# Three accumulation tables in place of four in a graph-layer kernel on one Trainium2 core

## The chip, the core and the metric

The kernel runs on one core of a Trainium2 chip. The core has five engines with instruction streams of their own: TensorE (PE, with its weight loads shown as PEld), VectorE (DVE), ScalarE (ACT), GpSimd (POOL) and SyncE (SP), and 16 DMA engines that they share. Semaphores order the streams. The metric is the device time of one execution in microseconds (us), lower is better. Times of several executions are given as a median; the profile is of one execution.

## What is computed

A layer over 6250 nodes of 256 features and 100000 edges, in float32. Three branches are added: a message-passing branch, a linear attention branch and, last, a slice-attention branch. The change touches the first one. Cut to what matters:

```python
xn = layernorm(x)
filt = silu(edge_attr @ Wf1 + bf1) @ Wf2 + bf2          # 100000 x 256
msg = xn[dst] * filt
agg = segment_sum(msg, src, num_segments=6250)          # scatter-add by src
h = silu(agg @ Wu1 + bu1) @ Wu2 + bu2
bn = gamma * (h - mean(h)) * rsqrt(var(h) + eps) + beta  # over the nodes
x = x + (xn + bn) + attention(xn)                        # then the slice branch
```

Edges come sorted by dst, so a row of `agg` (by src) is hit by edges from all over the list.

## The kernel before

Six stages run one after the other, each a block that ends with a barrier over the engines: `opening`, `messages_and_attention`, `update_nodes`, `slice_tokens`, `slice_attention`, `slice_output`.

**opening** normalises the rows of x, writes them split in two float32r halves to DRAM, and prepares the attention. Between those seven stores SP issues the clearing of the tables (L254 to L262): each table of 6400 rows of 256 floats in DRAM is cleared by 8 DMAs of 800 KB, 32 in all with four tables, four or five behind each store.

**messages_and_attention** (L716) goes over NCH = 98 chunks of 1024 edges, 8 tiles of 128 edges each, so 784 tiles; work is in pairs of tiles, 4 to a chunk. PE makes filter and gathered rows, DVE multiplies them to messages, PE sums messages of equal src within a tile, ACT copies the sums of a pair to `summed` (`copy_sums`, L1050, instruction on L1056), DVE makes the row indices `out_idx` (L1166), and POOL adds each tile's 128 rows of 1 KB to a table in DRAM with one indirect accumulating DMA (`scatter`, L893, instruction on L903). An accumulating DMA reads, adds and writes; two of them in flight on one table could lose a sum, as both may hit the same row. So tile t goes to table `t % 4`, and before its issue POOL waits (L902) on the semaphore `added[k]` until the scatter four tiles earlier, on the same table, has landed. `out_ready` and `sum_ready` (L894, L895) are waited for once a pair, before its first (even) tile.

`summed` has two buffers of 8 tiles. ACT may copy a pair only when the scatters of the same tiles two chunks earlier have landed (L1052 to L1055), so the sums can run at most 16 tiles ahead of the scatters. PE's next `merge` (L961) waits for that copy (`sum_ready`), and the rest of PE, ACT and DVE stands in order behind it.

The stage ends when all scatters have landed (L923). The attention's output is computed alongside, in the places of `output`.

**update_nodes** (L1268) takes 49 tiles of nodes in 13 units of four (the last has one). SP loads a unit's rows of all tables to `part` (L1352: 52 loads, 48 of 512 KB and 4 of 128 KB), two units deep. POOL adds part 2 and part 3 (`late_sums`, L1510 to L1513); DVE adds part 1 to part 0 (L1536), waits for POOL (L1538) and adds part 2 (L1539). PE turns the sum (L1375), multiplies by Wu1 (L1387) and, a unit behind, by Wu2 (L1401); POOL's other work is `low_hidden` (L1518), and ACT and DVE (L1550, statistics of h) finish the unit. The order on DVE is: sums of unit u+1, their low halves, statistics of unit u-1.

Of the kernel before, what the change touches and what calls it, by code (L numbers as in the profile page):

```python
# [24 lines left out]
NODES, C = 6250, 256  # L25
# [9 lines left out]
ET = 8  # L35
EC = ET * P
NCH = 2 * -(-EDGES // (2 * EC))
# [3 lines left out]
ROWS = -(-(PAD_SRC + 1) // P) * P  # L41
CLEARS = 8
HALF_RANGE = 63
TABLES = 4
FIRST_EXP = 127 + HALF_RANGE
SUM_STEPS = 3
X_PARTS = (0, 1, 3, 5)
# [69 lines left out]

def table_of(c, t):

    return t % TABLES  # L120

def added_by(k, c, t):

    return ET // TABLES * c + (t - k) // TABLES + 1

def row_moments(nc, dve, m, var, t0, n, step, base):
# [20 lines left out]
def opening(nc, sem, sb, g):  # L149
# [83 lines left out]
    with nc.Block() as block:  # L233
        @block.sync
        def _(sp):
# [17 lines left out]
            sp.wait_ge(filled, FILL_ZEROS)  # L253
            pieces = [(k, n) for n in range(CLEARS) for k in range(TABLES)]  # L254
            for k in range(NG):
# [437 lines left out]
def is_first(v):  # L693
    return isinstance(v, int) and v == 0
# [21 lines left out]
def messages_and_attention(nc, sem, sb, g):  # L716
# [26 lines left out]
    summed = [sb(f"summed{p}", [P, ET, XW], F32) for p in range(2)]  # L743
# [24 lines left out]
    out_ready = sem("e_out_ready")  # L768
    sum_made = sem("e_sum_made")
    sum_ready = sem("e_sum_ready")  # L770
    added = [sem(f"e_added{k}") for k in range(TABLES)]

    res = sb("res_stage", [P, GT, C], F32)
    r2 = sb("r2_rows", [GH, GC], F32)
# [27 lines left out]
    with nc.Block() as block:  # L802
# [73 lines left out]
        @block.gpsimd  # L876
        def _(pool):
            def gather(c, j):
                pool.wait_ge(gath_copied, PAIRS * c + j + 1)
                for t in range(2):  # L880
                    n = ET * c + 2 * j + t
                    nc.gpsimd.indirect_dma_start(
                        gathered[:, j, t, :], None, g.xhl_dram,
                        bass.IndirectOffsetOnAxis(ap=g.dst_all[:, n:n + 1], axis=0)).then_inc(wide_in, 16)
                pool.wait_ge(wide_in, 32 * (PAIRS * c + j + 1))
                for t in range(2):
                    n = ET * c + 2 * j + t
                    nc.gpsimd.indirect_dma_start(
                        gathered[:, j, t, :], None, g.xhl_dram,
                        bass.IndirectOffsetOnAxis(ap=g.dst_all[:, n:n + 1], axis=0), element_offset=C,  # L890
                        compute_op=ALU.add).then_inc(late_in[j], 16)

            def scatter(c, j):  # L893
                pool.wait_ge(out_ready, PAIRS * c + j + 1)  # L894
                pool.wait_ge(sum_ready, PAIRS * c + j + 1)  # L895
                for t in range(2 * j, 2 * j + 2):
                    k = table_of(c, t)
                    before = added_by(k, c, t) - 1
                    if is_first(c) and t < TABLES:
                        pool.wait_ge(g.table_clear[k], 16 * CLEARS)  # L900
                    else:
                        pool.wait_ge(added[k], 16 * before)  # L902
                    nc.gpsimd.indirect_dma_start(  # L903
                        g.sums_dram[k], bass.IndirectOffsetOnAxis(ap=out_idx[:, ET * c + t:ET * c + t + 1], axis=0),
                        summed[c % 2][:, t, 0:C], None, compute_op=ALU.add).then_inc(added[k], 16)

            is_wide = pool.value_load(g.wide_i[0:1, 0:1], min_val=0, max_val=1)
            with pool.If(is_wide > 0):
                gather(0, 0)
                gather(0, 1)  # L910
                for c in range(NCH):
                    for j in range(PAIRS):
                        n = PAIRS * c + j + 2
                        if n < NW:
                            gather(n // PAIRS, n % PAIRS)
                        scatter(c, j)
            with pool.Else():
                for j in range(PAIRS):
                    pool.sem_inc(late_in[j], 32 * NCH)
                for c in range(NCH):  # L920
                    for j in range(PAIRS):
                        scatter(c, j)
            for k in range(TABLES):  # L923
                pool.wait_ge(added[k], 16 * added_by(k, NCH - 1, ET - TABLES + k))

        @block.tensor
        def _(pe):
# [113 lines left out]
        def _(act):  # L1041
# [8 lines left out]
            def copy_sums(c, p, j):  # L1050
                act.wait_ge(sum_made, PAIRS * c + j + 1)
                if not (isinstance(c, int) and c < 2):  # L1052
                    for t in range(2 * j, 2 * j + 2):
                        k = table_of(c - 2, t)
                        act.wait_ge(added[k], 16 * added_by(k, c - 2, t))  # L1055
                A.activation(summed[p][:, ds(2 * j, 2), :], sps[:, :, 0:XW], ACT.Copy).then_inc(sum_ready, 1)  # L1056

            def high_attr(i, p):
# [19 lines left out]
            def chunk(i, p, last, work):  # L1078
                c = 2 * i + p
                for j in range(PAIRS):  # L1080
                    if j < PAIRS - 1:
                        copy_rows(c, j + 1)
                    elif not last:
                        copy_rows(c + 1, 0)
                    if j == 0 and not last:
                        high_attr(i + p, 1 - p)
                    if j == 0:
                        silu(c, 1, 1)
                    elif not last:
                        silu(c + 1, (j - 1) // 2, (j - 1) % 2)  # L1090
                    high_half(c, j)
                    if j:
                        copy_sums(c, p, j - 1)
                    elif not is_first(c):
                        copy_sums(c - 1, 1 - p, PAIRS - 1)
                    work(j)
# [20 lines left out]
            copy_rows(0, 0)  # L1117
            along(act, chunk, output)
            copy_sums(NCH - 1, 1, PAIRS - 1)

        @block.vector
# [126 lines left out]
UNITS = -(-NT // UT)  # L1248
# [3 lines left out]
def unit_tiles(u):  # L1252

    return range(u * UT, min(u * UT + UT, NT))
# [13 lines left out]
def update_nodes(nc, sem, sb, g):  # L1268
# [22 lines left out]
    weights_in = sem("u_weights_in")  # L1291
    res_in = sem("u_res_in")
    parts_in = [sem(f"u_parts_in{p}") for p in range(2)]
    two_ready, late_ready, agg_ready = sem("u_two_ready"), sem("u_late_ready"), sem("u_agg_ready")
    turned, turn_high, turn_low = sem("u_turned"), sem("u_turn_high"), sem("u_turn_low")
    wu_high, wu_low = sem("u_wu_high"), sem("u_wu_low")
    hid_made, hid_ready = sem("u_hid_made"), sem("u_hid_ready")
# [7 lines left out]
    part = [sb(f"part{p}", [P, TABLES, UT, C], F32) for p in range(2)]  # L1305
# [26 lines left out]
    def size(u):  # L1332
        return len(unit_tiles(u)) * P
# [13 lines left out]
    with nc.Block() as block:  # L1347
        @block.sync
        def _(sp):
            def load(u, k):  # L1350
                n = len(unit_tiles(u))
                sp.dma_start(part[u % 2][:, k, 0:n, :], split_rows(g.sums_dram[k], u * UT, n)).then_inc(parts_in[u % 2], 16)  # L1352

            for u in range(UNITS):
                if u >= 2:
                    sp.wait_ge(agg_ready, u - 1)
                for k in range(1, TABLES):
                    load(u, k)
                if u >= 2:
                    sp.wait_ge(turned, PAIRS_BEFORE[u - 1])  # L1360
                load(u, 0)
            half = NT // 2
            sp.dma_start(g.res[:, 0:half, :], split_rows(g.res_dram, 0, half)).then_inc(res_in, 16)
            sp.dma_start(g.res[:, half:NT, :], split_rows(g.res_dram, half, NT - half)).then_inc(res_in, 16)
# [141 lines left out]
        @block.gpsimd  # L1506
        def _(pool):
            G = nc.gpsimd

            def late_sums(u):  # L1510
                pool.wait_ge(parts_in[u % 2], 64 * (u // 2 + 1))
                c, d = (part[u % 2][:, k, 0:len(unit_tiles(u)), :] for k in (2, 3))
                G.tensor_tensor(c, c, d, ALU.add).then_inc(late_ready, 1)  # L1513

            def low_hidden(u, f):
                pool.wait_ge(hid_rounded, CB * u + f + 1)
                here = slice(0, size(u))
                G.tensor_tensor(hid_low[u % 2][:, f, here], hidT[u % 2][:, f, here],  # L1518
                                hid_high[u % 2][:, f, here].bitcast(F32), ALU.subtract).then_inc(hid_lowered, 1)

            late_sums(0)
            late_sums(1)
            for u in range(UNITS):
                for f in range(CB):
                    low_hidden(u, f)
                if u + 2 < UNITS:
                    late_sums(u + 2)

        @block.vector
        def _(dve):  # L1530
            V = nc.vector

            def gather_sums(u):
                dve.wait_ge(parts_in[u % 2], 64 * (u // 2 + 1))
                a, b, c = (part[u % 2][:, k, 0:len(unit_tiles(u)), :] for k in range(3))
                V.tensor_tensor(a, a, b, ALU.add).then_inc(two_ready, 1)  # L1536
                dve.wait_ge(two_ready, u + 1)
                dve.wait_ge(late_ready, u + 1)  # L1538
                V.tensor_tensor(a, a, c, ALU.add).then_inc(agg_ready, 1)  # L1539

            def low_sums(u):
# [644 lines left out]
```

## Time and profile before

| what | value |
|---|---|
| median of 3 runs | 2218.55 us (2213.65 to 2227.55) |
| the profiled execution, its own time | 2221.49 us |
| its span in the trace | 2219.7 us |
| mean granted TensorE clock | 0.944 |
| busy: PE / DVE / ACT / POOL | 1924.0 / 1528.4 / 1307.3 / 1441.2 us |
| instructions | 38972 |
| DMA traffic | 325.45 MB, mean 147 GB/s |

The span is from the first to the last instruction. Busy time is an average over six stages with different limits, so the large share of PE does not by itself say what sets the time of a stage. POOL's time is nearly all on one line, L903. In the rows further down, a group of instructions shows its line, engine, operation, what it writes <- what it reads, the count, busy us, mean ns of one, and the idle time of the engine just before them with what ended it. "issue" means that nothing the profile shows was waited for.

### The profile page before, as it was taken

How to read it: one execution, taken by the hardware profiler on the slowest of the kernel's cores; microseconds unless marked ns; L12 is line 12 of the kernel's file. 1: busy time of each engine (PE TensorE's matmuls, PEld its weight loads, DVE VectorE, ACT ScalarE, POOL GpSimd, SP SyncE). 2: the span in 40 equal slices, each digit the busy share in tenths (PEclk: the TensorE clock that was granted, in tenths of full speed). 3: DMA queues.
4: the chain of work that ended last, by engine and by line, in shares of the span. 5: the costliest groups of instructions: out<-in, count | busy, mean ns of one | idle time of the engine just before them, and what ended most of it. 6: DMA issues, size and time to landing. Idle time of an engine off the chain costs nothing. (4 is left out here: it accounts for less than half of the span.)

```text
span 2219.7 us, 38972 instructions
## 1 busy us (share of the span) xinstructions
PE 1924.0 (87%) x10218; PEld 1587.5 (72%) x10218; DVE 1528.4 (69%) x3525; ACT 1307.3 (59%) x2330; POOL 1441.2 (65%) x989
## 2 busy tenths in 40 slices
PE   3687999989999989998899989998990785999878
PEld 2466788778877777777777777777780574788678
DVE  6654777777767767776776677767771557999645
ACT  2333776767666667666776676667760463666423
POOL 2111888888888888888888888888885550455300
PEclk9898999999999999999999999999995895999979
DMA  8656888988898888888988888798886880000002
GB/s 276 275 225 204 160 157 153 187 147 149 146 180 155 149 157 169 145 153 158 171 155 151 173 160 155 141 184 156 143 132 121 263 277 0 1 0 0 20 20 97
DMA packets 288441, 325.45 MB, mean 147 GB/s; under 512 B 29575, under 2 KB 251178, under 8 KB 288146
## 3 DMA queue, kind: packets, MB, share of 16 engines
q0 software_dynamic: 112896, 102.81, 37.7%
q1 hardware_dynamic: 169568, 216.13, 30.9%
q10 hardware_dynamic: 5746, 3.90, 0.7%
q8 instruction: 88, 1.44, 0.3%
q14 instruction: 143, 1.17, 0.2%
HBM read 167.64 MB, written 154.97 MB: 145 GB/s over the span
## 5 line engine op out<-in xcount | busy, mean ns | idle before, releaser
L903 POOL DMA_INDIRECT sums<-summed,out_idx x784 | 1238.8, 1580 | 295.7 <-issue 208.3
L957 PE MATMUL bank<-wf,hidT 128*128 128x256 f32 x3136 | 802.0, 384 | 0.0
L957 PEld LDWEIGHTS bank<-wf,hidT 128*128 128x128 f32 x3136 | 547.2, 192 | 54.7
L1048 ACT ACTIVATE hidT<-bank,bf 128x512 f32<-128x512 f32 x392 | 269.8, 688 | 265.4 <-PE bank L935 222.3
L1143 DVE TENSOR_TENSOR msg_low<-msg,msg_high 128x512 fp32r<-128x512 f32 x392 | 271.9, 694 | 175.0 <-ACT msg_high L1068 129.0
L1174 DVE TENSOR_TENSOR msg<-bank,gathered 128x512 f32<-128x512 f32 x392 | 269.2, 687 | 117.6 <-PE bank L957 91.6
L1068 ACT ACTIVATE msg_high<-msg 128x512 fp32r<-128x512 f32 x392 | 247.3, 631 | 92.2 <-DVE msg L1174 79.1
L955 PE MATMUL bank<-gnn_bf_halves,ones 128*128 128x256 f32 x784 | 298.2, 380 | 0.0
L1056 ACT ACTIVATE summed<-pair 128x516 f32<-128x516 f32 x392 | 230.3, 588 | 61.6 <-DMA sums<-summed,out_idx 59.1
L1075 ACT ACTIVATE gathered<-bank 128x512 f32<-128x512 f32 x392 | 231.9, 592 | 49.8 <-issue 22.3
L945 PE MATMUL bank<-window,spread 128*128 128x256 f32 x784 | 194.6, 330 | 62.6 <-DVE spread L1138 38.3
L935 PE MATMUL bank<-attr_parts,wf_parts 128*128 128x512 f32 x392 | 225.2, 574 | 26.0 <-DVE attr_parts L1128 22.0
L969 PE MATMUL pair<-msg_high,same 128*128 128x258 f32 x784 | 209.5, 289 | 23.6 <-ACT summed L1056 14.1
L945 PEld LDWEIGHTS bank<-window,spread 128*128 128x128 f32 x784 | 124.9, 191 | 126.5 <-issue 85.4
L969 PE MATMUL pair<-msg_low,same 128*128 128x258 f32 x784 | 206.6, 284 | 0.0
L969 PEld LDWEIGHTS pair<-msg_high,same 128*128 128x128 f32 x784 | 149.8, 191 | 47.4 <-issue 19.2
L1138 DVE TENSOR_TENSOR spread<-id_row,half_f 128x256 fp32r<-128x256 uint8 x392 | 165.2, 422 | 26.3 <-issue 17.6
L1153 DVE TENSOR_TENSOR same<-id_row,src_f 128x256 fp32r<-128x256 int16 x392 | 162.2, 414 | 0.0
L969 PEld LDWEIGHTS pair<-msg_low,same 128*128 128x128 f32 x784 | 149.2, 190 | 15.4
L955 PEld LDWEIGHTS bank<-gnn_bf_halves,ones 128*128 128x128 f32 x784 | 150.9, 193 | 10.8
L1163 DVE SCALAR_TENSOR_TENSOR redirect<-summed,first_limit,to_trash 128x2 f32<-128x2 f32 x392 | 85.5, 218 | 61.3 <-ACT summed L1056 48.6
L935 PEld LDWEIGHTS bank<-attr_parts,wf_parts 128*128 128x128 f32 x392 | 75.4, 192 | 61.9 <-issue 36.1
(324 smaller groups left out, 2823.4 us busy)
## 6 DMA issues: line engine op xcount, KB each, us to landing
window<-xn_halves SPq DMA_DIRECT2D x392, 128.0 KB
sums<-gate SPq DMA_DIRECT2D x32, 800.0 KB, 10.1
id_row<-id_rows SPq DMA_DIRECT2D x98, 256.0 KB
attr<-attr_rows SPq DMA_DIRECT2D x98, 256.0 KB
part<-sums SPq DMA_DIRECT2D x48, 512.0 KB, 6.6
xn_halves<-xn_halves SPq DMA_DIRECT2D x7, 1792.0 KB, 6.6
id_row<-id_rows SPq DMA_DIRECT2D x98, 128.0 KB
sums<-summed,out_idx POOLq DMA_INDIRECT x784
```

Source lines behind the costliest of these rows:

```text
L903: nc.gpsimd.indirect_dma_start(g.sums_dram[k], bass.IndirectOffsetOnAxis(ap=out_idx[:, ET * c + t:ET * c + t + 1], axis=0), summed[c % 2][ ...
L935: T.matmul(hps[:], g.wf1_parts[:, h, ds(f * P, P)], attr_parts[:, p, :], start=True, stop=True).then_inc(hid_made, 1)
L945: mm = T.matmul(gps[:, ds(t * C, C)], spread[:, j % 2, ds(t * P, P)], window[:, j, :], start=True, stop=True)
L955: T.matmul(out, g.ones2[:], g.bf2[:], start=True, stop=False)
L957: mm = T.matmul(out, hidT[:, j // 2, f, ds((2 * (j % 2) + t) * P, P)], g.wf2[:, f, :], start=False, stop=f == CB - 1)
L969: mm = T.matmul(sps[:, t, 0:XW], same[:, p, 2 * j + t, :], half[:, j % 2, t, :], start=k == 0, stop=k == 1)
L1048: A.activation(hidT[:, h, f, :], hps[:], ACT.Silu, bias=g.bf1[:, f:f + 1]).then_inc(hid_ready, 1)
L1056: A.activation(summed[p][:, ds(2 * j, 2), :], sps[:, :, 0:XW], ACT.Copy).then_inc(sum_ready, 1)
L1068: A.activation(msg_high[:, j % 2, :, 0:C], msg[:, j % 2, :, :], ACT.Copy).then_inc(high_ready, 1)
L1075: A.activation(gathered[:, j, :, :], gps[:].rearrange("p (t c) -> p t c", c=C), ACT.Copy).then_inc(gath_copied, 1)
L1143: V.tensor_tensor(msg_low[:, j % 2, :, 0:C], msg[:, j % 2, :, :], msg_high[:, j % 2, :, 0:C].bitcast(F32), ALU.subtract).then_inc(low_read ...
L1174: V.tensor_tensor(msg[:, j % 2, :, :], fps[j % 2][:].rearrange("p (t c) -> p t c", c=C), gathered[:, j, :, :], ALU.mult).then_inc(msg_read ...
```

## The change

`TABLES` goes from 4 to 3. The table of a tile is `(8 c + t) % 3`, so tiles take the tables in turn over all chunks, and a scatter waits for the landing of the scatter three tiles earlier. The landing counts get their own number of semaphores, `ADDED = 4`, one for each tile place modulo 4, so that their counts stay simple. `copy_sums` waits for the same scatters as before. The opening clears three tables (24 DMAs), `update_nodes` loads three parts (39 DMAs), `late_sums` on POOL is gone, and DVE adds the third part without waiting for POOL. The table count of the buffers `part` and `sums` follows.

```diff
-TABLES = 4
+TABLES = 3
+ADDED = 4
...
 def table_of(c, t):
-    return t % TABLES
-def added_by(k, c, t):
-    return ET // TABLES * c + (t - k) // TABLES + 1
+    return (ET * c + t) % TABLES
...
-    added = [sem(f"e_added{k}") for k in range(TABLES)]
+    added = [sem(f"e_added{k}") for k in range(ADDED)]
...
                     k = table_of(c, t)
-                    before = added_by(k, c, t) - 1
-                    if is_first(c) and t < TABLES:
+                    before = ET * c + t - TABLES
+                    if before < 0:
                         pool.wait_ge(g.table_clear[k], 16 * CLEARS)
                     else:
-                        pool.wait_ge(added[k], 16 * before)
+                        pool.wait_ge(added[before % ADDED], 16 * (before // ADDED + 1))
                     nc.gpsimd.indirect_dma_start(
                         g.sums_dram[k], bass.IndirectOffsetOnAxis(ap=out_idx[:, ET * c + t:ET * c + t + 1], axis=0),
-                        summed[c % 2][:, t, 0:C], None, compute_op=ALU.add).then_inc(added[k], 16)
+                        summed[c % 2][:, t, 0:C], None, compute_op=ALU.add).then_inc(added[t % ADDED], 16)
...
-            for k in range(TABLES):
-                pool.wait_ge(added[k], 16 * added_by(k, NCH - 1, ET - TABLES + k))
+            for k in range(ADDED):
+                pool.wait_ge(added[k], 16 * (ET // ADDED) * NCH)
...
-                        k = table_of(c - 2, t)
-                        act.wait_ge(added[k], 16 * added_by(k, c - 2, t))
+                        act.wait_ge(added[t % ADDED], 16 * (ET // ADDED * (c - 2) + t // ADDED + 1))
...
-            def late_sums(u):
-                pool.wait_ge(parts_in[u % 2], 64 * (u // 2 + 1))
-                c, d = (part[u % 2][:, k, 0:len(unit_tiles(u)), :] for k in (2, 3))
-                G.tensor_tensor(c, c, d, ALU.add).then_inc(late_ready, 1)
...
-            late_sums(0)
-            late_sums(1)
             for u in range(UNITS):
                 for f in range(CB):
                     low_hidden(u, f)
-                if u + 2 < UNITS:
-                    late_sums(u + 2)
...
             def gather_sums(u):
-                dve.wait_ge(parts_in[u % 2], 64 * (u // 2 + 1))
+                dve.wait_ge(parts_in[u % 2], 16 * TABLES * (u // 2 + 1))
                 a, b, c = (part[u % 2][:, k, 0:len(unit_tiles(u)), :] for k in range(3))
                 V.tensor_tensor(a, a, b, ALU.add).then_inc(two_ready, 1)
                 dve.wait_ge(two_ready, u + 1)
-                dve.wait_ge(late_ready, u + 1)
                 V.tensor_tensor(a, a, c, ALU.add).then_inc(agg_ready, 1)
```

## Rows read from the trace of the kernel before

**Rows 1.** Busy time by stretch of the span; columns in the first line.
```profile
core 0: us, PE busy (x) PEld busy (x) DVE busy (x) ACT busy (x) POOL busy (x), PEclk, DMA share, GB/s
900.00:1300.00 400.00, 368.89 (x1917) 306.54 (x1916) 281.47 (x683) 269.69 (x463) 332.58 (x211) 0.98 0.86 159
```

**Rows 2.** One line's instructions, L903: duration min/median/max, first and last start.
```profile
L903 POOL DMA_INDIRECT sums<-summed,out_idx x784: 1538/1540/2055, 212.1 to 1700.8; - x196
...
  DMA sums<-summed,out_idx: 32.0, 69
```

**Rows 3.** Groups of instructions from the start to 912.6 us.
```profile
L903 POOL DMA_INDIRECT sums<-summed,out_idx x366 | 581.4, 1589 | 164.0 <-issue 97.3 <-DVE out_idx L1166 47.0 <-DMA sums<-summed,out_idx 16.3
L1056 ACT ACTIVATE summed<-pair 128x516 f32<-128x516 f32 x190 | 111.4, 586 | 20.4 <-DMA sums<-summed,out_idx 19.8 <-issue 0.4
```

**Rows 4.** Waits of POOL from 300 to 1670 us: total, times, longest.
```profile
POOL sums L903 <- issue: 191.8, 624, 0.6
POOL sums L903 <- DMA sums<-summed,out_idx: 29.6, 66, 2.6
POOL sums L903 <- ACT summed L1056: 6.7, 22, 0.3
POOL sums L903 <- DVE out_idx L1166: 3.3, 10, 0.5
```

**Rows 5.** Scatters in order of time: start, duration, [idle before <- releaser].
```profile
417.78 1.54 POOL L903 DMA_INDIRECT sums<-summed,out_idx  x1 [0.30 <-issue]
420.93 1.54 POOL L903 DMA_INDIRECT sums<-summed,out_idx  x1 [1.61 <-DMA sums<-summed,out_idx]
...
839.09 1.69 POOL L903 DMA_INDIRECT sums<-summed,out_idx  x1 [0.30 <-issue]
841.09 1.66 POOL L903 DMA_INDIRECT sums<-summed,out_idx  x1 [0.30 <-issue]
843.05 1.56 POOL L903 DMA_INDIRECT sums<-summed,out_idx  x1 [0.30 <-DVE out_idx L1166]
844.91 1.72 POOL L903 DMA_INDIRECT sums<-summed,out_idx  x1 [0.30 <-issue]
849.28 1.54 POOL L903 DMA_INDIRECT sums<-summed,out_idx  x1 [2.65 <-DMA sums<-summed,out_idx]
```

**Rows 6.** Stretches around the last scatter, which starts at 1700.84; columns as rows 1.
```profile
1701.00:1702.40 1.40, 0.00 (x0) 0.00 (x0) 0.00 (x0) 0.00 (x0) 1.39 (x1) 0.50 0.81 94
1703.40:1704.40 1.00, 0.00 (x0) 0.00 (x0) 0.00 (x0) 0.00 (x0) 0.00 (x0) 0.50 0.66 102
1704.40:1705.40 1.00, 0.00 (x0) 0.00 (x0) 0.00 (x0) 0.00 (x0) 0.00 (x0) 0.50 0.00 0
```

**Rows 7.** End of the opening in order of time.
```profile
168.35 6.82 SPq L239 DMA_DIRECT2D sums<-gate  x5
...
188.71 0.69 DVE L632 COPY wqm<-bank 128x512 f32<-128x512 f32 x1 [1.25 <-PE bank L382]
```

**Rows 8.** SP's wait for DMAs from 160 to 200 us: total, times, longest.
```profile
SPq L269 <- DMA wf_parts<-wf_high: 1.4, 1, 1.4
```

**Rows 9.** First units of update_nodes in order of time.
```profile
1719.17 1.22 DVE L1536 TENSOR_TENSOR part<-part 128x1024 f32<-128x1024 f32 x1 [11.23 <-DMA part<-sums]
1722.70 1.22 DVE L1539 TENSOR_TENSOR part<-part 128x1024 f32<-128x1024 f32 x1 [2.31 <-POOL part L1513]
...
1729.12 1.23 DVE L1536 TENSOR_TENSOR part<-part 128x1024 f32<-128x1024 f32 x1 [1.50 <-DMA part<-sums]
...
1732.68 1.23 DVE L1539 TENSOR_TENSOR part<-part 128x1024 f32<-128x1024 f32 x1 [2.33 <-POOL part L1513]
1733.96 1.10 PE L1375 MATMUL bank<-ident,part 128*128 128x128 f32 x8 [1.06 <-DVE part L1539]
...
1740.14 1.23 DVE L1539 TENSOR_TENSOR part<-part 128x1024 f32<-128x1024 f32 x1 [2.33 <-POOL part L1513]
```

**Rows 10.** A later unit of update_nodes in order of time.
```profile
1756.70 1.21 DVE L1536 TENSOR_TENSOR part<-part 128x1024 f32<-128x1024 f32 x1
1757.94 1.22 DVE L1539 TENSOR_TENSOR part<-part 128x1024 f32<-128x1024 f32 x1
...
1764.45 1.21 DVE L1536 TENSOR_TENSOR part<-part 128x1024 f32<-128x1024 f32 x1
```

More of the change, by code:

```diff
@@ L1293, in update_nodes @@
     parts_in = [sem(f"u_parts_in{p}") for p in range(2)]
-    two_ready, late_ready, agg_ready = sem("u_two_ready"), sem("u_late_ready"), sem("u_agg_ready")
+    two_ready, agg_ready = sem("u_two_ready"), sem("u_agg_ready")
     turned, turn_high, turn_low = sem("u_turned"), sem("u_turn_high"), sem("u_turn_low")
```

## The prediction

> **What bounds the kernel now.** I read the table of stretches first. From 900 to 1300 us, the middle of the message stage, PE is busy for 368.9 of 400 us at a granted clock of 0.98, and POOL computes for 332.6 us; neither is full, so the shares alone don't say who sets the pace [rows 1].
>
> The view of one line's instructions comes next, for POOL's scatters. There are 784, 1.54 us each in the median; the first starts at 212.1 and the last at 1700.8 us [rows 2]. That is (1700.8 - 212.1) / 783 = 1.901 us a tile. Two scatters that follow each other at once are 1.54 + 0.30 = 1.84 us apart; the 0.30 stands before every scatter, also where the releaser is only "issue" [rows 5]. Durations above 1.54 lift the mean to 1.58 [rows 3], so 1.88 us a tile is POOL's own pace and 0.02 is left for waiting.
>
> The groups up to 912.6 us show who is ahead. ACT has started 190 copies of pairs, the last of them at that moment, so 380 tiles; POOL has issued 366 scatters [rows 3]. POOL is 14 tiles behind with a ring of 16, and ACT's idle time there is charged to the landing of scatters (19.8 us). The ring is full, so POOL sets the pace of the stage and PE, ACT and DVE wait behind it. The table of waits agrees: POOL never waits for data. Its waits for ACT (22 times, 6.7 us) and DVE (10 times, 3.3 us) are the ordinary 0.30 us gap [rows 4]. What is added between two scatters therefore lengthens the stage one for one, and nothing can hide it.
>
> **The change part by part.**
>
> *The wait before a scatter.* Tile n waited for the landing of n-4 and now waits for n-3. This is the only edit on POOL's path. Today 69 waits end on a landing, 32.0 us [rows 2]; less the ordinary gap that is 32.0 - 69 x 0.30 = 11.3 us, and going through all scatters in order I find 22 that were really held up, two of which stand in [rows 5]. The one at 849.28 had its partner, four scatters back, end at 839.09 + 1.69 = 840.78, so it landed as much as 849.28 - 0.30 - 840.78 = 8.2 us after that end; undelayed scatters must have landed within about 5.5 us.
>
> With three tables the budget from the end of a scatter to the moment its successor on the table is ready to start shrinks by one period, to two periods and a gap: 2 x 1.88 + 0.30 = 4.06 us.
>
> Lower bound: only the landings that are too late today are too late then, each by one period more: 22 x 1.845 = +41 us.
>
> Upper bound: the landings between the old and new budget count too. No view prints when a scatter lands, but the trace holds the records of the semaphore increments. For 779 scatters I took the last increment before the table's next use, counted from the end of the POOL instruction: 5% by 2.2 us, half by 2.95, mean 3.27, 90% by 4.65, 99% by 6.1, longest 7.7. The table of stretches confirms the low end: after the last scatter ends at about 1702.4 nothing else runs, and the DMA engines are quiet from 1704.4, so it landed about 2 us after its end [rows 6]. The rest of a landing is queueing behind window and id loads, with the DMA engines 0.86 busy [rows 1]. The same records show what a release costs: 0.27 us from landing to start for the second tile of a pair and 0.76 us for the first, which passes a separate wait instruction. I replayed the sequence: start = the later of (end of the last scatter + 0.305) and (landing of the partner + 0.27 or 0.76), with each scatter's own duration and landing delay. With partners four back it gives 22 delays and 12.7 us, the trace's own 22 delays. With partners three back it gives 193 delays and 128.1 us: +115 us.
>
> The truth should be between. The replay keeps every landing as late as today, though held-up scatters meet a DMA load that is spread thinner (5% more time for the same bytes); the lower bound supposes that all middling lateness goes. Both ends have about the same claim, so I take the middle, +78 us.
>
> Here a rule of the Trainium skill speaks for hiding the wait. The page "DMA: Bandwidth & Descriptors", section "Anatomy of one DMA — SWDGE (gpsimd) path", fits a GpSimd-issued DMA as 2.0 us plus bytes over 436e3, which for a tile's 128 KB is an estimated 2.3 us, almost constant. By it the trimmed budget would never be exceeded and this term would be 0. The trace agrees only for the unloaded landing [rows 6]; the held scatters contradict it [rows 5].
>
> What queues behind the waiting scatter: the next scatters only. ACT's copies (L1052) and behind them PE and DVE wait for the ring, which is full already, so their loss is the same microseconds and not more.
>
> *The tables' clearing.* Eight clears of 800 KB go. SP issues the last five at 168.35 and DVE's last work of the opening ends at 188.71 + 0.69 = 189.4 [rows 7]; SP's only wait for earlier DMAs in that tail is 1.4 us [rows 8]. The clears run under the opening's compute. Bounds 0 and -1.4; I take -0.5. If this cover were gone, 6.5 MB would cost more, but nothing here takes it away.
>
> *The added-semaphores and copy_sums.* Same instructions with the same targets: 0.
>
> *update_nodes.* Loads fall from 52 to 39 and POOL's adds go. At the start this is on the path. Unit 0's sum waits 11.23 us for its parts and 2.31 us for POOL; unit 1's waits 1.50 us for parts and 2.33 us for POOL [rows 9]. Both units' loads are issued together, so by unit 1 a quarter of the bytes, 1 MB of 4, is missing. From the wait's start (1707.9) to unit 1's parts at 1729.1 are 21 us, of which the missing quarter would be up to 5. PE then takes over: it turned unit 1 at 1733.96 and was busy with unit 0 until shortly before. I take -5 us. Lower bound of the gain: one POOL wait, -2.3. Upper: 3 x 2.3 plus the 1.5 us wait, about -8. From 1756.70 on no sum waits for DMA or POOL; units follow each other every 1764.45 - 1756.70 = 7.75 us with the two adds of 1.21 and 1.22 us back to back [rows 10]. They stay two adds, so nothing changes there.
>
> *Sum.* 78 - 0.5 - 5 = +72.5 us on the span of 2219.7 us gives 2292. That span's execution ran 2221.49 us against the median 2218.55, so medians come out about 1 us below spans: 2291 us. Ends: +41 - 1.4 - 8 = +32, so 2250; +115 - 2.3 = +113, so 2331.
>
> **The rivals.**
>
> *A. The forecast:* the three-deep chain delays POOL 100 to 200 times. For it: the full ring and the 22 delays. Against: lateness may shrink. 2291 us, 2250 to 2331.
>
> *B. Not slower:* the scatters land in time. The late landings come from bursts of loads; were they a matter of those 22 cases alone and their shift moved them out of the bursts, the wait would cost nothing and the savings of 5.5 us stay: 2218.55 - 5.5 = 2213 us. It decides if landings stay under about 3.3 us (first tile of a pair) and 3.8 us (second). Against it: 32.0 us of waiting even with a budget a period longer [rows 2]. The page's fit leads here.
>
> *C. The clock falls:* PE now works 368.9 us for 211 scatters [rows 1], 1.75 us a tile at clock 0.98. If stalls brought the mean clock to 0.80, PE would need 1.75 x 0.98 / 0.80 = 2.14 us a tile and overtake POOL's 2.0 as the bound: 784 x (2.14 - 1.90) = +188, less 5.5: about 2401 us. It decides below a clock of about 0.86. Before, with the ring full too, the clock stays at 0.98, which speaks against it.
>
> *D. Lateness grows* because delayed scatters fall into later bursts or because three more delays in a row feed each other beyond the replay: every scatter on the first place of a pair held for 0.5 us more gives 392 x 0.5 = 196 us, less 5.5: about 2409 us. Only the size speaks: the replay has half of that.
>
> *E. The change does not do what it says:* the table sequence is computed in Python for each unrolled scatter, so this can't be beyond a slip in the counts; no chance of its own.
>
> **How the numbers follow.** A 0.82, B 0.08, C 0.04, D 0.06. Within A 0.02 may fall below its lower and 0.02 above its upper bound, since both rest on one execution. The predicted time is A's, 2291 us. The range 2250 to 2333 us holds the remaining 0.78 of A and, at its edges, a little of the others; B below it and C and D above it are the 2 in 10 left out. One per cent (22 us), about what a measurement can tell here, is 2196 and 2241. Slower is A, C and D without most of the slack under A's lower bound: 0.90. Within 1% is B, mostly, and that slack: 0.08. Faster would need a gain of over 22 us where the savings make at most 9.4: 0.02.
>
> **What would show it.** The same line's view: 1.54 us a scatter unchanged, the first start near 212, the last near 1700.8 + 78 = 1779, some 100 to 190 waits on landings of well over 100 us in all with the gaps. The gap of first tiles of pairs should hold most of it. The groups up to mid-stage should again show ACT about 14 tiles ahead; if not, POOL is no longer the bound and the step "one for one" is wrong. In update_nodes no DVE wait for POOL, the first sum 2 to 3 us after the barrier earlier, the unit time 7.75 us as before. A last scatter near 1700 us would sink the whole argument; a granted clock below 0.9 in the stage would point to C.

## The result and the profile after

The changed kernel is slower: 2346.9 us median (2331.31 to 2353.45, 4 runs) against 2219.87 us (2213.65 to 2227.55, 4 runs), a ratio of 1.056 with a 95% interval of 1.0496 to 1.0625. The direction was forecast; the size was not. 2291 us was predicted, with 2333 us as the upper end.

The profiled execution has a span of 2341.1 us, 121.4 more than before. The difference lies almost wholly between the first and the last scatter. This is the view of one line's instructions for POOL's scatters, now L899, in the changed kernel (count, duration ns min/median/max, first and last start; below, idle time and times by releaser).

```profile
L899 POOL DMA_INDIRECT sums<-summed,out_idx x784: 1538/1540/2048, 211.5 to 1828.1; - x196
...
  issue: 147.6, 479
  ACT summed L1051: 135.3, 120
  DMA sums<-summed,out_idx: 74.6, 120
  DVE out_idx L1161: 67.2, 65
```

| part of the span | before | after | difference |
|---|---|---|---|
| up to the first scatter | 212.1 | 211.5 | -0.6 |
| first to last scatter | 1488.7 | 1616.6 | +127.9 |
| from the last scatter on | 518.9 | 513.0 | -5.9 |

The median duration of a scatter stays 1540 ns as in [rows 2]; what grows is the idle time before them. The releaser must be read with care. POOL seems to wait for ACT 120 times, 135.3 us, where in the whole kernel before it was 23 times and 7.0 us (22 of them stand in [rows 4]). But ACT is ahead. These are the changed kernel's groups up to 1200 us (count, busy, mean ns, idle before and its releasers):

```profile
L899 POOL DMA_INDIRECT sums<-summed,out_idx x479 | 754.8, 1576 | 278.3 <-issue 88.8 <-ACT summed L1051 80.7 <-DVE out_idx L1161 56.8
L1051 ACT ACTIVATE summed<-pair 128x516 f32<-128x516 f32 x246 | 145.2, 590 | 126.6 <-DMA sums<-summed,out_idx 125.1 <-issue 1.0
```

246 copies are 492 tiles against 479 scatters: 13 tiles behind, the ring still nearly full, as in [rows 3]. ACT's own idle time there is 125.1 us on landings. One landing releases both: ACT's copy of a much later pair, and POOL's next scatter. The copy's own signal then falls into POOL's gap and takes the label. The real cause is the landing: by the records of its increments, 95 of the 108 held first tiles of pairs start 0.76 us after the landing three tiles back, to within 2 ns.

The stretch in the middle of the stage, in the columns of [rows 1]:

```profile
900.00:1300.00 400.00, 353.32 (x1768) 285.17 (x1766) 262.70 (x637) 252.25 (x433) 306.28 (x195) 0.97 0.79 144
```

By their counts of instructions all engines do 6 to 8% less in the 400 us (PE's busy time falls by 4% only). The DMA share is 0.79 against 0.86, and the granted clock 0.97 against 0.98.

What a delay looks like is in the changed kernel's order of time for POOL (start, duration, idle before). 971.09 is the first tile of a pair; its partner three back is the scatter that starts at 963.06.

```profile
963.06 1.54 POOL L899 DMA_INDIRECT sums<-summed,out_idx  x1 [0.30 <-issue]
964.90 1.54 POOL L899 DMA_INDIRECT sums<-summed,out_idx  x1 [0.30 <-issue]
966.75 1.81 POOL L899 DMA_INDIRECT sums<-summed,out_idx  x1 [0.30 <-issue]
971.09 1.54 POOL L899 DMA_INDIRECT sums<-summed,out_idx  x1 [2.53 <-ACT summed L1051]
```

And these are SP's issues around it, from the same view:

```profile
962.23 0.33 SPq L806 DMA_DIRECT2D id_row<-id_rows  x1
963.53 0.19 SPq L814 DMA_DIRECT2D window<-xn_halves  x1
963.82 0.38 SPq L802 DMA_DIRECT2D id_row<-id_rows  x1
965.49 0.34 SPq L814 DMA_DIRECT2D window<-xn_halves  x1
966.15 0.33 SPq L810 DMA_DIRECT2D attr<-attr_rows  x1
967.42 6.55 SPq L814 DMA_DIRECT2D window<-xn_halves  x2
...
980.44 0.33 SPq L806 DMA_DIRECT2D id_row<-id_rows  x1
```

From 962.23 to 967.42 SP issues 128 + 128 + 256 + 128 + 256 + 128 KB, 1024 KB of a chunk's 1152 KB, in 5 us; the next such clump begins 18 us later. The scatter of 963.06 falls into it (by the records it landed 5.7 us after its end), and the successor that waits for it is held 2.23 us beyond the ordinary gap of 0.30.

The gains are there too. In update_nodes of the changed kernel (order of time):

```profile
1844.28 1.22 DVE L1522 TENSOR_TENSOR part<-part 128x1024 f32<-128x1024 f32 x1 [9.11 <-DMA part<-sums]
1845.53 1.23 DVE L1524 TENSOR_TENSOR part<-part 128x1024 f32<-128x1024 f32 x1
```

The first sum waits 9.11 us for its parts where it was 11.23, and its second add follows at once, where it waited 2.31 us for POOL [rows 9].

No view prints when a scatter lands. As in the prediction, the numbers on landings below come from the trace's records of semaphore increments, and "delay" is the gap before a scatter beyond 0.305 us, summed over gaps above 0.35 us. One execution stands behind each. The traces hold 77 to 93% of these increments; where the last of a landing is missing, the landing reads too early.

| kernel | stage, us a tile | delays, us (count) | landing after the scatter's end: mean | DMA share 900 to 1300 us |
|---|---|---|---|---|
| before | 1.901 | 12.7 (23) | 3.27 | 0.86 |
| changed | 2.065 | 142.5 (143) | 3.19 | 0.79 |

So 129.8 us of delays are added and 2.0 us come off the durations (784 x 2.6 ns): 127.8 of the stage's 127.9.

### The profile page after: what moved, and what is told of

Its sections match the earlier page's. It is cut to its first block and busy times, and to the rows that moved or that the text cites. A ratio compares the mean times of both kernels' runs of the same rounds, so it can differ in the third digit from the quotient of the medians.

```text
span 2341.1 us, 38925 instructions
## 1 busy us (share of the span) xinstructions
PE 1967.6 (84%) x10218; PEld 1599.9 (68%) x10218; DVE 1531.1 (65%) x3525; ACT 1308.7 (56%) x2330; POOL 1406.9 (60%) x976
## 5 line engine op out<-in xcount | busy, mean ns | idle before, releaser
L899 POOL DMA_INDIRECT sums<-summed,out_idx x784 | 1236.7, 1577 | 424.6 <-issue 147.6
L953 PE MATMUL bank<-wf,hidT 128*128 128x256 f32 x3136 | 815.9, 389 | 0.0
L953 PEld LDWEIGHTS bank<-wf,hidT 128*128 128x128 f32 x3136 | 557.3, 196 | 57.7
L951 PE MATMUL bank<-gnn_bf_halves,ones 128*128 128x256 f32 x784 | 302.9, 386 | 0.0
L965 PE MATMUL pair<-msg_high,same 128*128 128x258 f32 x784 | 215.7, 296 | 88.1 <-ACT summed L1051 82.0
L941 PE MATMUL bank<-window,spread 128*128 128x256 f32 x784 | 201.2, 339 | 81.2 <-DVE spread L1133 37.6
```

The lines of the kernel that those rows point to most:

```text
L899: nc.gpsimd.indirect_dma_start(g.sums_dram[k], bass.IndirectOffsetOnAxis(ap=out_idx[:, ET * c + t:ET * c + t + 1], axis=0), summed[c % 2][ ...
L941: mm = T.matmul(gps[:, ds(t * C, C)], spread[:, j % 2, ds(t * P, P)], window[:, j, :], start=True, stop=True)
L951: T.matmul(out, g.ones2[:], g.bf2[:], start=True, stop=False)
L953: mm = T.matmul(out, hidT[:, j // 2, f, ds((2 * (j % 2) + t) * P, P)], g.wf2[:, f, :], start=False, stop=f == CB - 1)
L965: mm = T.matmul(sps[:, t, 0:XW], same[:, p, 2 * j + t, :], half[:, j % 2, t, :], start=k == 0, stop=k == 1)
```

## The experiments

The theory: the whole loss is POOL's wait for a landing that now is three tiles back, and landings are about as late as they were, because clumps of loads hold them up. The rivals: something about the three tables themselves; lateness from the scatters' own traffic or from the mean load; a fixed cost of the stage's rhythm.

### Four tables, wait three back

```diff
-                    before = added_by(k, c, t) - 1
+                    before = ET * c + t - 3
...
-                        pool.wait_ge(added[k], 16 * before)
+                        pool.wait_ge(added[before % 4], 16 * (before // 4 + 1))
```

> The kernel before, four tables and all, but each scatter waits for the landing three tiles earlier in place of four. Theory 1 (the loss is only the shorter wait on POOL's path): stage from first to last scatter 1616 us as in the changed kernel, about 140 us of delays, and the whole about 5 us above the changed kernel, since clears, loads and POOL's adds stay: about 2350 us. Theory 2 (part of the loss comes from the three tables themselves, their turn over the tiles or their places in DRAM): well under that, 2330 us or less.

Measured: 2353.53 us, ratio to the kernel before 1.0581 (1.055 to 1.0613). The line's view of this kernel:

```profile
L903 POOL DMA_INDIRECT sums<-summed,out_idx x784: 1539/1541/2044, 214.0 to 1834.9; - x196
```

1620.9 us from first to last scatter, 148.1 us of delays. The wait alone makes all of the loss; three tables as such add nothing to a stage that is 1616.6 us with them. Above the changed kernel it lies by 6.6 us of median, about the 6.5 us of gains that the spans show, though the two intervals overlap.

### Only three parts in update_nodes

```diff
-                for k in range(1, TABLES):
+                for k in range(1, 3):
...
-                dve.wait_ge(late_ready, u + 1)
```

POOL's `late_sums` and its calls go as well.

> The kernel before with scatters into four tables, but update_nodes loads and adds three of them (left out: the fourth table's sums). It isolates what update_nodes gains. My step said 5 us (2.3 to 8): 2215 us, stage of scatters unchanged at 1.90 us a tile. The rival, that the first units wait on something other than parts and POOL, gives 0.

Measured: 2217.62 us, ratio 0.9978 (0.9962 to 0.9994), so 1 to 8 us less, 4 to 5 in the middle. In its trace the second add again follows at once (order of time):

```profile
1719.01 1.23 DVE L1527 TENSOR_TENSOR part<-part 128x1024 f32<-128x1024 f32 x1 [8.88 <-DMA part<-sums]
1720.27 1.22 DVE L1529 TENSOR_TENSOR part<-part 128x1024 f32<-128x1024 f32 x1
```

The step of -5 us holds.

### Fewer bytes beside the scatters

```diff
-                sp.dma_start(window[:, j, :].bitcast(F32), g.xhl_dram[ds(base, P), :])...
+                n = C if isinstance(c, int) and c < 1 else 16
+                sp.dma_start(window[:, j, 0:n].bitcast(F32), g.xhl_dram[ds(base, P), 0:n])...
```

The loads of offsets and attributes are cut in the same way.

> The changed kernel with all loads of windows, offsets and edge attributes after the first chunks cut to a few columns (left out: most of that data, so messages are of stale rows). Of 1.15 MB a chunk 0.27 MB is left. Theory 1 with lateness from clumped loads: landings nearly all near 2.2 us, under 20 us of delays, stage back to about 1.89 us a tile, and about 2215 us in all. Rival (lateness comes from the scatters' own reading and writing in DRAM): delays stay above 70 us, 2280 us or more.

Measured: 2247.69 us, ratio 1.0109 (1.0063 to 1.0154), 99 us under the changed kernel. Mean landing 2.60 us, 52.5 us of delays (79). Its stretch:

```profile
900.00:1300.00 400.00, 363.84 (x1889) 302.80 (x1888) 278.35 (x675) 261.94 (x455) 321.08 (x206) 0.98 0.72 99
```

Neither expectation was met exactly. Most of the added delay, 90 of 130 us, goes with the loads' bytes. A rest stays, with 304 KB a chunk still loaded of 1152 (the source ids are whole, so it is not the 0.27 MB of the expectation).

The trace's records of DMA packets tell what goes with this rest. For each scatter, the table counts what SP's queue moved beside it: the bytes of its packets that started from 1.5 us before to 2.2 us after the end of the POOL instruction. The delays are those of the scatters that wait three back for the scatters counted.

| moved beside the scatter | changed kernel: scatters, mean landing, delays | fewer bytes: scatters, mean landing, delays |
|---|---|---|
| under 50 KB | 125, 2.25 us, 0 us | 471, 2.31 us, 2.2 us |
| 50 to 200 KB | 308, 2.60 us, 4.7 us | 112, 2.53 us, 6.6 us |
| 200 to 400 KB | 57, 3.39 us, 23.3 us | 167, 3.15 us, 28.1 us |
| 400 KB and more | 291, 4.17 us, 114.5 us | 31, 4.40 us, 15.5 us |

In the changed kernel 138 of the 142.5 us of delays follow scatters that had 200 KB or more beside them; here it is 44 of 52.5 us. Scatters with hardly any load beside them land after 2.3 us and hold nothing up, so the scatters' own traffic alone accounts for some 2 us. The table by itself shows only what goes together; that the bytes are the cause rests on the edit.

### Wait two back

```diff
-                    before = added_by(k, c, t) - 1
+                    before = ET * c + t - 2
```

The wait itself reads as in the first experiment.

> The kernel before with each scatter waiting for the landing two tiles earlier. The replay of landing records gives 714 us of delays in place of 12.7: about 2920 us if landings stay as late as they are. If lateness thins as scatters spread out, all scatters still pay for the fixed part: with every landing at 2.2 us the replay would give about 0.8 us before each first tile of a pair and 0.2 before each second, about 400 us: 2610 us.

Measured: 2754.72 us in one execution (no interval). 543.9 us of delays, between the two numbers expected. (The lower one was too high by its own working: with every landing at 2.2 us, a first tile's 0.76 us after the landing is 0.77 us more than the ordinary way to it, and second tiles then wait for nothing: 392 x 0.77 = 302 us and not 400.) Its stretch:

```profile
900.00:1300.00 400.00, 311.42 (x1419) 240.94 (x1419) 212.28 (x508) 200.35 (x343) 246.72 (x156) 0.92 0.65 113
```

Here landings do come earlier, 2.79 us in the mean at a DMA share of 0.65. So lateness thins with the load, but hardly yet for a stage that is only 9% longer: 3.27, 3.19, 2.79 us at shares of 0.86, 0.79, 0.65.

### One wait less before a pair

```diff
                 pool.wait_ge(out_ready, PAIRS * c + j + 1)
-                pool.wait_ge(sum_ready, PAIRS * c + j + 1)
```

> The changed kernel without the wait for sum_ready before a pair's first scatter, which the wait for out_ready implies. If then the wait for the landing sits on the scatter itself for both tiles of a pair, a release costs 0.27 us everywhere; the replay of the changed kernel's landings gives 103 us of delays in place of 141: about 2309 us. Rival (the 0.76 us is not the separate wait instruction): no change, 2347 us.

> The same edit in the kernel before. The replay gives 7 us of delays in place of 12.7: 5 us less, 2214 us. Rival: no change.

Measured: changed kernel with the edit 2339.69 us, ratio 1.0536 (1.0502 to 1.057), which overlaps the changed kernel's 1.0496 to 1.0625; kernel before with it 2220.92 us, ratio 0.9983 (0.9968 to 0.9998).
### The landing's wait named first

```diff
-                pool.wait_ge(out_ready, PAIRS * c + j + 1)
-                pool.wait_ge(sum_ready, PAIRS * c + j + 1)
                 for t in range(2 * j, 2 * j + 2):
...
                         pool.wait_ge(added[before % ADDED], 16 * (before // ADDED + 1))
+                    if t == 2 * j:
+                        pool.wait_ge(out_ready, PAIRS * c + j + 1)
+                        pool.wait_ge(sum_ready, PAIRS * c + j + 1)
```

> The changed kernel with the order of a pair's first waits turned round: first the landing, then out_ready and sum_ready. The earlier edit left the landing's wait on an instruction of its own and its release at 0.73 us. If the first wait named is the one that rides on the scatter, all releases are 0.27 us now, and the replay of the changed kernel's landings gives 103 us of delays in place of 141: about 2310 us. Rival (the extra half microsecond belongs to a pair's first tile whatever the order): 2347 us.

> The same order in the kernel before. The replay gives 7 us of delays in place of 12.7: 5 us less than the kernel before, about 2217 us beside 2222. Rival: no change.

Measured: changed kernel with the turned order 2308.35 us, ratio 1.0384 (1.0353 to 1.0414), against 1.0496 to 1.0625 without it. All releases are 0.27 us, and delays are 100.6 us (125); 103 was expected. Its line's view, with the label now where it belongs:

```profile
L900 POOL DMA_INDIRECT sums<-summed,out_idx x784: 1538/1540/2057, 211.5 to 1796.7; - x196
...
  DMA sums<-summed,out_idx: 141.1, 137
  DVE out_idx L1162: 48.7, 16
  ACT summed L1052: 7.5, 21
```

In the kernel before, the same order gives 2211.04 us, ratio 0.9957 (0.994 to 0.9973), 6 to 13 us less than before, where 5 were expected. It is the fastest of the kernels here that leave nothing out. Delays are 2.3 us, where the replay said 7, and the landing's idle time is down from the 32.0 us and 69 times of [rows 2] in its line's view:

```profile
L904 POOL DMA_INDIRECT sums<-summed,out_idx x784: 1539/1541/2061, 212.0 to 1686.2; - x196
...
  DMA sums<-summed,out_idx: 7.4, 17
```

### Loads spread over the chunk

```diff
-                    if j == 2 and goes_on:
-                        sp.wait_ge(spread_ready, PAIRS * (c + 1))
-                        load_offsets(c + 2, p)
-                    if j == 3 and goes_on:
-                        sp.wait_ge(same_ready, PAIRS * (c + 1))
-                        load_src(c + 2, p)
                     if not last:
                         sp.wait_ge(gath_made, PAIRS * c + j + 1)
                         load_window(c + 1, j)
+                    if j == 2 and goes_on:
+                        load_src(c + 2, p)
+                    if j == 3 and goes_on:
+                        load_offsets(c + 2, p)
```

> The changed kernel with SP's loads of source ids and offsets moved behind the windows of pairs 2 and 3 of a chunk, without the waits of their own that held SP up (the window's wait implies them), so that a chunk's loads are spread over more of its time. Theory 1 with lateness from clumps: late landings fall, delays drop from 142 us to 60 to 110, 2270 to 2315 us. Rival (lateness follows the mean load): no change, as the bytes are the same.

> The same move of loads in the kernel before. There only 12.7 us of delays are left to win: 5 to 10 us less, about 2212 us, if landings come earlier; 2220 us if not.

> Both edits in the changed kernel, the turned order of waits and the spread loads. The replay of the spread kernel's landings with 0.27 us at every release gives 74 us of delays in place of 116: about 2310 - 40 = 2270 us. If the two gain from the same late landings, no better than 2300 us.

Measured: changed kernel with spread loads 2310.24 us, ratio 1.038 (1.0346 to 1.0415), within the time expected; delays 115.9 us, just above the 60 to 110 expected; mean landing 3.06. Same bytes, less lateness, at a DMA share that is higher (0.83 against 0.79), so it is when the loads come and not only how many bytes they are. The spread was a partial one: SP still issued 768 KB within 3.5 us (from 970.25 to 973.48 us). With both edits 2277.23 us, ratio 1.0247 (1.0226 to 1.0268), delays 77.2 us where the replay said 74. In the kernel before the spread alone does nothing: 2223.26 us, ratio 1.0004 (0.999 to 1.0018). There its delays stay at 12.6 us, though the mean landing falls to 3.18 us. The expectation tied a gain of 5 to 10 us to earlier landings and was wrong: the mean fell, the late tail did not (99% landed by 6.1 us in both kernels).

### Five tables

Against the kernel before, cut; the rest follows the changed kernel.

```diff
-TABLES = 4
+TABLES = 5
+PARTS = 4
+ADDED = 8
...
```

> Scatters into five tables, each waiting for the landing five tiles earlier; the opening clears five, and update_nodes adds four of them as before (left out: the fifth table's sums; two semaphores are shared to make room). The replay gives no delays in place of 12.7 us: stage at 1.885 us a tile, about 10 to 12 us under the kernel before, 2211 us. Rival (POOL's own durations grow to fill what is won, or the clears cost): 2222 us.

Measured: 2210.24 us, ratio 0.9942 (0.9923 to 0.9962), and not one delay. Its line's view:

```profile
L901 POOL DMA_INDIRECT sums<-summed,out_idx x784: 1540/1540/2055, 214.3 to 1691.2; - x196
```

1476.9 us for the stage is 1.886 us a tile, POOL's own pace as the prediction worked it out. The 11.7 us of median that it gains (8 to 17 by the interval) are about the 12.7 us of delays that four tables still have. The kernel leaves out the fifth table's sums. A fifth part to load and add would have to be paid in update_nodes, where the fourth costs 4 to 5 us, so five tables would probably win less than this; that was not run.

The scatters' delays against the distance of the wait, where only that distance decides:

| wait for the landing of | 2 back | 3 back | 4 back | 5 back |
|---|---|---|---|---|
| delays, us | 543.9 | 148.1 | 12.7 | 0 |

## Why the prediction was right and wrong

**POOL sets the pace, and added gaps count one for one: right.** 127.8 us of gaps and durations against 127.9 us of stage. The ring is nearly full in the changed kernel as before.

**The direction and the mechanism: right.** The wait three back makes the loss by itself (2353.53 us with four tables).

**The size of the wait: wrong, and this is the step that failed.** The term was +78 us, the middle between +41 (only today's 22 late landings) and +115 (the replay of the landing records); it measured +129.8. Two things went wrong in it.

First, the choice of the middle. It was argued with a DMA load spread thinner. The load did get thinner, 0.79 against 0.86, but the mean landing fell by 0.08 us only. Late landings go with clumps of loads once a chunk, and the longer chunk has such a clump still, with a longer pause behind it. The lower bound needed nearly all middling lateness to vanish; nothing in the rows supported that, and the replay should have been the estimate. This choice made 37 of the 52 us that were missing.

Second, the replay was treated as an upper bound. It was none: 142.5 us of delays came, 128.1 were replayed. The rule of the replay is not at fault: fed with the changed kernel's own landings it gives 141 us. The landings changed. The replay keeps each tile's lateness at its place in the chunk. In the kernel before the mean landing was latest at places 4, 5 and 6 of the 8, counted from 0 (3.73, 3.93, 3.55 us); in the changed kernel at 3, 4 and 5 (4.08, 4.08, 3.61). By the kernel's waits SP's issues follow PE, PE follows the ring and the ring follows POOL, so the clump can keep a place among the tiles, and that place can shift. The successor of place 3 is place 6, the first tile of a pair, whose release costs 0.76 us and not 0.27: that one place took 90.5 of the 142.5 us. That the place moved is read from the records; why it moved by one was not tested. Nor is the shift enough: with the old landings moved one place ahead the replay gives 131 us, 64 of them at place 6. So it makes about 3 of the 14 us; the others go with landings at places 3 and 4 that are later than any place's were before (4.08 against 3.93 us at most), and their cause stays open.

**The release of 0.76 and 0.27 us: right as numbers, and worth more than thought.** First tiles of pairs had 108 of the 143 delays. Turning the waits' order took 42 us of delays and 39 us of median from the changed kernel.

**The savings: right.** Opening -0.6 against -0.5 us; after the last scatter -5.9 against -5 us; the experiment gave the second 4 to 5 us.

**The rivals.** B, not slower, needed landings under 3.3 and 3.8 us; they are not, and 10% are above 4.8 us. The fit of the page "DMA: Bandwidth & Descriptors" of the Trainium skill (section "Anatomy of one DMA — SWDGE (gpsimd) path"), 2.3 us as an estimate, agrees with the earliest tenth of landings, about 2.2 us, and not with a mean of 3.2 us among other traffic. The 2.2 us are counted from the end of the POOL instruction, as in the prediction; from its start they are 3.8 us. C, the clock: the granted clock is 0.97 from 900 to 1300 us, so no; only the wait two back brings it to 0.92. D, growing lateness, priced 196 us; the replay was exceeded, but by 14 us, and whether delays feeding on each other had a part in them was not tested.

**The range.** Its upper end was the replay less the least gain (2331 us in the sum, 2333 in the range as stated). It left out that the replay itself rests on the landings of one kernel, and that those could come later at some places. One reading was slightly off: the mean duration of 1.58 us is that of all scatters; the group in [rows 3] has 1.589. It changes nothing in the term that failed.

## What to carry to other kernels

Here an engine with a full ring in front of it paced a stage, and its waits for its own transfers cost one for one. A replay with their landing times came within 14 us of the 142.5 us of delays; the middle between two bounds missed by 52 us. Cutting the chain from four deep to three cost 130 us to save 6, because the depth paid for the late tail of landings and not for their mean.
## What the runs showed of the hardware

- A 128 KB accumulating scatter landed 2.25 us after its POOL instruction's end in the mean with under 50 KB of SP's transfers beside it, and 4.17 us with 400 KB or more (changed kernel). Over all scatters the mean was 3.2 to 3.3 us at a DMA share of 0.79 to 0.86, and 2.8 us at 0.65. Taking away 848 of the 1152 KB of loads in each chunk brought it from 3.19 to 2.60 us.
- Spreading the same loads over the chunk raised the DMA share from 0.79 to 0.83 and cut the delays from 142.5 to 115.9 us: the mean share does not tell how late a transfer is.
